# A transformer layer with routed experts: the opening norm stage in a new order, and the first maxima scheduled anew

## The reference, cut to what matters

```python
x = x + _layernorm(attn(_layernorm(x)))          # x is 4 batches x 1024 tokens x 256
x = x + _layernorm(ffn(_layernorm(x)))           # 8 experts, one per token

def attn(x):
    latent = x @ Wc_down                          # 256 -> 128
    q = (latent @ Wq_up).reshape(B, T, 16, 16)    # 16 heads of 16
    k, v = split(latent @ Wkv_up)                 # one key and one value head for all
    att = softmax(causal(q @ k.T / 4))
    return (att @ v) @ Wc_proj

def ffn(x):                                       # logits = x @ centroids.T, argmax picks the expert
    ...
```

## Time and profile before

| | |
|---|---|
| median of 3 runs | 882.81 us (882.48 to 886.35) |
| the profiled execution | 882.63 us, of which 880.9 us span |
| PE busy | 825.6 us (94%) |
| DVE busy | 638.9 us (73%) |
| ACT busy | 550.7 us (63%) |
| POOL busy | 292.9 us (33%) |
| TensorE clock, mean granted | 0.963 of full |
| first maximum on PE | 45.62 us from the span's start |
| first score on PE | 60.60 us |

### The profile page before, as it was taken

One profiled execution on the slowest core, in us unless ns is written; L12 is line 12 of the kernel. 1 busy time (PEld: TensorE's weight loads), 2 busy tenths in 40 slices (PEclk: granted clock), 3 DMA queues, 4 the chain that ended last, 5 costly groups with the idle time before them and its releaser, 6 DMA issues. The chain is left out here.

```text
span 880.9 us, 20297 instructions
## 1 busy us (share of the span) xinstructions
PE 825.6 (94%) x5520; PEld 495.3 (56%) x5521; DVE 638.9 (73%) x2133; ACT 550.7 (63%) x1244; POOL 292.9 (33%) x547
## 2 busy tenths in 40 slices
PE   7999999999999999999999999469999999999993
PEld 3533333333433333433333338369999999999993
DVE  7789889898888898898988607835555555555552
ACT  3624768777766777676776876146666666666661
POOL 4502322443244233432233322042444444444211
PEclk9977999999999999999999999669999999999997
DMA  6111233222311111111143228920000100110000
GB/s 204 42 40 62 80 99 107 76 71 89 106 58 48 40 60 52 55 35 56 56 152 100 71 76 251 334 96 25 30 31 31 35 29 27 36 32 23 21 19 1
DMA packets 55764, 62.92 MB, mean 71 GB/s; under 512 B 13166, under 2 KB 47366, under 8 KB 55568
## 3 DMA queue, kind: packets, MB, share of 16 engines
q1 hardware_dynamic: 51952, 53.71, 18.7%
q0 software_dynamic: 3744, 8.40, 3.1%
HBM read 36.12 MB, written 9.57 MB: 52 GB/s over the span
## 5 line engine op out<-in xcount | busy, mean ns | idle before, releaser
L1066 ACT ACTIVATE W2s<-bank 128x512 f32<-128x512 f32 (+1 forms) x512 | 257.2, 572 | 126.1 <-PE bank L978 123.8
L1116 DVE CUSTOM_DVE_ANT_0 room_kv<-bank,causal 128x384 bf16<-128x384 f32 (+3 forms) x512 | 220.6, 485 | 31.4 <-PE bank L947 29.8
L978 PE MATMUL bank<-W2s,room_kv 99*128 99x512 bf16 (+3 forms) x768 | 225.8, 331 | 5.1 <-ACT W1s L1066 3.3
L947 PE MATMUL bank<-room_kv,W2s 96*128 96x512 bf16 (+3 forms) x768 | 222.8, 336 | 4.3 <-DVE R L1088 3.0
L1119 DVE TENSOR_REDUCE MP<-bank 128x1 f32<-128x512 f32 x256 | 162.9, 680 | 13.6 <-PE bank L947 13.5
L1248 POOL TENSOR_SCALAR_AFFINE_SELECT W2s<-W2s 128x512 f32<-128x512 f32 x96 | 61.2, 637 | 291.4 <-ACT W2s L1066 289.3
L978 PEld LDWEIGHTS bank<-W2s,room_kv 99*128 99x128 bf16 x768 | 68.2, 98 | 146.4 <-ACT W2s L1066 64.6
L1516 PEld LDWEIGHTS hp<-XNT,LT 128*128 128x128 f32 x1248 | 148.0, 195 | 3.7 <-DVE XNT L1593 1.8
L1516 PE MATMUL hp<-XNT,LT 128*128 128x128 f32 x1248 | 148.5, 278 | 1.4 <-DVE XNT L1593 1.4
L1524 PE MATMUL yp<-W2s,LT 128*128 x624 | 141.2, 379 | 0.7 <-DVE z L1605 0.7
L995 PE MATMUL bank<-W2s,room_kv 128*32 128x512 f32 (+2 forms) x1152 | 128.6, 531 | 0.2 <-ACT W1s L1052 0.2
(11 more groups left out here) (185 smaller groups left out, 777.7 us busy)
## 6 DMA issues: line engine op xcount, KB each, us to landing
W2s<-W2s SPq DMA_DIRECT2D x160, 64.0 KB, 2.6
W1s<-in_L_ffn_W_dram SPq DMA_DIRECT2D x8, 1024.0 KB, 5.6
W2s<-in_L_ffn_W_dram SPq DMA_DIRECT2D x8, 1024.0 KB, 7.2
Y<-in_L_attn_x_dram SPq DMA_DIRECT2D x8, 512.0 KB, 6.2
Y<-W1s SPq DMA_DIRECT2D x32, 128.0 KB
W1s<-den_rows SPq DMA_DIRECT2D x16, 256.0 KB
LT<-in_L_attn_x_dram SPq DMA_DIRECT2D x8, 512.0 KB, 6.5
x_rows<-LT SPq DMA_DIRECT2D x8, 512.0 KB, 4.2
```

The costliest lines, as they stand in the source:

```text
L947: last = pe.matmul(bank[:, at:at + w], Q[0:NR, g, i // BW, h, i % BW * P:(i % BW + 1) * P], K[b % 2][0:NR, k * NQ:k * NQ + w], start=True, ...
L978: last = pe.matmul(dst[:, i, :], K[b % 2][0:KR, j * P:(j + 1) * P], Q[0:KR, g, c, h, off:NQ], start=True, stop=True)
L1066: act.activation(PR[t % RB][:, heads[0]:heads[-1] + 1, off:NQ], unit_of(ST[(NU * n + u) % STB], s), ACT.Exp, scale=SCALE).then_inc(exp_don ...
L1116: op = dve.tensor_tensor_reduce(junk[:, done % 2, at:at + w], src, causal[:, NQ - w:NQ], 1.0, LOWEST, ALU.add, ALU.max, dst)
```

## The change

The eight tiles of the norm stage are no longer a loop. Each engine gets a written-out order:

- the norm of tile 1 goes directly behind that of tile 0 and the norm of tile 2 directly behind its statistics; `down` of tiles 0 and 1 follows tile 1's transposes;
- "k" is the first piece and "q00" the second, both after tile 2; "q01" after tile 3, "q10" after tile 4, "q11" after tile 5;
- `XT` has five buffers instead of three;
- `down` of tile 6 goes to before event 4, `x_parts` of batch 2 to before event 7, its `x_fold` to before event 10; `down` of tile 7, `x_parts` and `x_fold` of batch 3 go behind the first scores of round 0 (steps 0, 1 and 2);
- the schedule: 20 maxima before the first score instead of 22, 45 at x = 10 instead of 48, and only at the end of the round the lead of 38; in round 0 an "m" lies 2 maxima behind its chunk's last one instead of 5; the first values lie at 18.2 instead of right behind the first chunk's maxima.

```diff
-FIRST = ("q00", "k", "q01", "q10", "q11")
-FIRST_AT = {2: ("q00",), 3: ("k", "q01"), 4: ("q10", "q11")}
+FIRST = ("k", "q00", "q01", "q10", "q11")
...
-EARLY = 22
+EARLY = 20
+MIDDLE = 45
 MLAT = 5
+FIRST_MLAT = 2
...
     def reached(x):
-        return EARLY + x * (c0 + LEAD - EARLY) / c0 if x < c0 else x + LEAD
+        if x < c0:
+            return EARLY + x * (MIDDLE - EARLY) / c0
+        return MIDDLE + (x - c0) * (c1 + LEAD - MIDDLE) / (c1 - c0) if x < c1 else x + LEAD
...
-            marks.append((NM * r + SET_LAST[c] + MLAT + 0.5, ("m", r, c)))
-    marks.append((SET_LAST[0] + 0.3, ("values", 0, None)))
+            marks.append((NM * r + SET_LAST[c] + (MLAT if r else FIRST_MLAT) + 0.5, ("m", r, c)))
+    marks.append((EARLY - 1.8, ("values", 0, None)))
...
+            statistics(0, 0)
+            statistics(1, 1)
+            inverse(0, 0)
+            norm(0)
+            inverse(1, 1)
+            norm(1)
+            statistics(2, 2)
+            inverse(2, 2)
+            norm(2)
+            statistics(3, 0)
+            centre()
+            remainder("k")
+            remainder("q00")
+            inverse(3, 0)
+            norm(3)
+            remainder("q01")
+            statistics(4, 1)
...
+            turn(0)
+            turn(1)
+            down(pe, 0)
+            down(pe, 1)
+            turn(2)
+            first("k")
+            first("q00")
+            down(pe, 2)
+            turn(3)
+            first("q01")
+            c_turn()
+            down(pe, 3)
+            x_parts(pe, 0)
+            turn(4)
+            first("q10")
+            x_fold(pe, 0)
+            down(pe, 4)
+            turn(5)
+            first("q11")
+            x_parts(pe, 1)
+            down(pe, 5)
+            turn(6)
+            x_fold(pe, 1)
+            turn(7)
...
                 if k == 2:
-                    down(pe, N1 - 1)
-                    x_parts(pe, B - 1)
-                    pe.wait_ge(lx_done, B - 1)
+                    pe.wait_ge(lx_done, B - 2)
                 if k == 3:
-                    pe.wait_ge(lt_copied, N1)
-                if k == FOLD_AT:
-                    x_fold(pe, B - 1)
+                    pe.wait_ge(lt_copied, N1 - 2)
+                if k == LATE_AT:
+                    down(pe, N1 - 2)
+                if k == PARTS_AT:
+                    pe.wait_ge(xt_copied, N1)
+                    x_parts(pe, B - 2)
+                if k == PARTS_AT + 3:
+                    x_fold(pe, B - 2)
                 event(k)
...
+                    if n == 0 and s == 0:
+                        down(pe, N1 - 1)
+                    if n == 0 and s == 1:
+                        pe.wait_ge(lt_copied, N1)
+                        x_parts(pe, B - 1)
+                    if n == 0 and s == 2:
+                        x_fold(pe, B - 1)
```

More of the change, by code:

```diff
@@ L471, in remainder, with norm @@
                 dve.tensor_tensor(rest, bank, parts(name)[0], ALU.subtract).then_inc(first_left, 1)
[L473 to L476, removed]
+            def norm(t):
                 dve.wait_ge(rstd, t + 1)
@@ L480, in norm_vector @@
                     normalise(dve, t, i).then_inc(xn_dve, 1)
[L481 to L491, removed]
+            statistics(0, 0)
[15 more added lines that the diff above has]
+            statistics(4, 1)
+            inverse(4, 1)
+            norm(4)
+            statistics(5, 2)
+            statistics(6, 0)
+            inverse(5, 2)
+            norm(5)
+            remainder("q10")
+            x_logits(dve, 0)
+            statistics(7, 1)
+            inverse(6, 0)
+            norm(6)
+            remainder("q11")
+            inverse(7, 1)
+            norm(7)
+            x_logits(dve, 1)
         def down(pe, t):
@@ L525, in norm_tensor, with turn @@
             pe.wait_ge(w_in, 48)
-            for t in range(N1):
+            def turn(t):
+                past(pe, xt_copied, t - 1)
                 for i in range(QT):
@@ L536, in norm_tensor, with first, c_turn @@
                 last.then_inc(xt_ready, 1)
[L537 to L546, removed]
-                    x_fold(pe, t // 2 - 1)
-                for name in FIRST_AT.get(t, ()):
-                    i, bank, _ = spot(name)
-                    if i == 0:
-                        pe.wait_ge(wq_turned, 1)
-                    pe.wait_ge(lt_copied, QC if name == "k" else int(name[-1]) + 1)
-                    past(pe, first_left, i - 1)
-                    piece(pe, 0, name, bank).then_inc(first_ready, 1)
+            def first(name):
+                i, bank, _ = spot(name)
+                pe.wait_ge(wq_turned, 1)
+                pe.wait_ge(lt_copied, QC)
+                past(pe, first_left, i - 1)
+                piece(pe, 0, name, bank).then_inc(first_ready, 1)
+            def c_turn():
+                pe.wait_ge(c_step, 3)
+                for c in range(DC):
+                    last = pe.transpose(lxp[0][:, c * E:(c + 1) * E], Cn[:, c * P:(c + 1) * P], ident[0:E, 0:E])
+                last.then_inc(c_turned, 1)
+            turn(0)
[22 more added lines that the diff above has]
+            turn(7)
         def norm_scalar(act):
@@ L599, in norm_scalar @@
-            latent(N1 - 1, (N1 - 1) % 2)
-            x_copy(B - 1)
+            turned(0)
+            turned(1)
+            root(2, 2)
+            latent(0, 0)
+            latent(1, 1)
+            turned(2)
+            root(3, 0)
+            first("k")
+            first("q00")
+            second("k")
+            second("q00")
+            latent(2, 0)
+            turned(3)
+            first("q01")
+            root(4, 1)
+            second("q01")
+            c_copy()
+            latent(3, 1)
@@ L602, in attention @@
+            x_copy(0)
+            turned(4)
+            root(5, 2)
+            root(6, 0)
+            first("q10")
+            latent(4, 0)
+            second("q10")
+            turned(5)
+            root(7, 1)
+            first("q11")
+            x_copy(1)
+            second("q11")
+            latent(5, 1)
+            turned(6)
+            turned(7)
+            latent(6, 0)
+            x_copy(2)
+            return latent, x_copy
         PR = [W2s[:, 4 + k, :].rearrange("p (h q) -> p h q", h=GH) for k in range(RB - 1)]
```

100 lines of the change are left out of this document (54 added, 46 removed).

## The result

| | before | changed |
|---|---|---|
| median | 883.43 us (9 runs, 882.48 to 888.41) | 890.00 us (9 runs, 885.15 to 890.13) |
| ratio | | 1.0053, 95% interval 1.0034 to 1.0071 |
| the profiled execution | 882.63 us | 890.07 us (span 888.3) |
| TensorE clock, mean granted | 0.963 | 0.959 |
| first maximum on PE | 45.62 us | 43.00 us |

The change makes the kernel about 0.5% slower; the interval leaves out 1. (The two medians alone are 0.74% apart and the means of the nine runs 0.48%: a median of runs that lie in groups jumps between them.) 882.81 (the median that the forecast was made against) times 1.0053 is 887.5, within the range of 878 to 889; the changed kernel's own median of 890.0 is 1.0 above its end. The forecast of 884.6 had the sign and underestimated the size.

What follows compares the result with a forecast made beforehand. DVE was taken to bound the catching up of the maxima. Start 43.0 + work 50.1 + 0.2 + idle 8.4 put round 0's end at 101.7 against 99.8, 1.9 us later: 884.6 us, range 878.0 to 889.0.

Steps and rivals of the forecast that it cites:

- term 1: End of the norm stage: first maximum on PE at 43.0 us instead of 45.62; bounds 40.3 and 45.6.
- Gap and logit sums (2, 3): DVE's gap at 49.29: 0.4 of 1.80 us stays; batch 2's logit sums behind the maxima: 0.2 more work.
- First "m" (4): Round 0, behind chunk 0's maxima: DVE stops for 0.9 us; bounds 0 and 1.3.
- Values (5): First values, near 56 us: 3.3 us at low clock, DVE idle 1.8 us; bounds 0.1 and 2.0.
- `down` of tile 7 (6): Among round 0's first scores: DVE idle 1.8 us, clock halfway back; bounds 0.1 and 3.3.
- Second "m" (7): Behind chunk 1's maxima: DVE idle 2.1 us in place of 0.26, plus 0.3 for batch 3's logit sums.
- "0.5 stays" (8): Last 8 steps of round 0: three moved maxima fill DVE's idle 1.45 us, of which 0.5 stays.
- Rival 3: Clock stays low through all three float32 pieces among the scores: 889.6 us, chance 0.10.
- Rival 1: Clock stays high through the values and `down`, 0.1 us idle at each: 881.2 us, chance 0.24.
- Rival 2: SP's transfers set the start at 40.3 us and the "m"s cost little: 876.5 us, chance 0.12.
- Rival 4: Start not earlier, at 45.6 us, since DVE's waits for ACT pile up: 887.2 us, chance 0.06.

Runs made afterwards that it cites:

- e9: The changed kernel with round 0's first "m" 5 maxima behind its chunk again, the second still 2: 887.90 us, 1.0029 to the kernel before.
- e5: The changed kernel with round 0's second "m" 5 maxima behind its chunk again, the first still 2: 881.56 us, 0.9967 to the kernel before.
- e1: The changed kernel with both of round 0's "m"s 5 maxima behind their chunks again: 881.38 us, 0.9980 to the kernel before.
- e10: e12 with two extra float32 products on PE ahead of each "m" of round 0: 882.23 us, 0.9977 to the kernel before.
- e12: The changed kernel with both "m"s 5 maxima behind and the values at their old place: 879.52 us, 0.9941 to the kernel before.
- e7: The changed kernel with two extra float32 products on PE ahead of each "m" of round 0: 883.43 us, 1.0004 to the kernel before.
- e4: The kernel before, with its old norm order, given only the new schedule: 888.42 us, 1.0051 to the kernel before.

## Why the prediction was right, and where it was short

**Start (term 1): right, and to the digit by luck.** 43.0 forecast, 43.00 measured, with the keys' first part at 18.05 (18.9 forecast) and SP waiting 3.5 us for "q01" (2 forecast). The forecast lay between 42.3 with the clock high and 43.8 with it low early. The clock did not fall at 13.9, with the new order in no trace; here it fell at 23.7. Where it stayed high in the norm stage, nine traces show 42.05 to 42.30, so the count of the work was good within 0.3 us.

**Gap and logit sums (2, 3): right, if anything too large.** DVE has no wait over 0.3 us between 43.56 and 52.44, for 0.4 forecast.

**First "m" (4): right at its place, short in effect.** Its rows show 0.88 + 0.32 = 1.20 for 0.9; e9 and e5 price it at 1.5 to 2.3 in round 0.

**Values (5): right.** 3.60 us and a wait of 1.90, for 3.3 and 1.8. The clock was low, and that was the step most in doubt. Not foreseen: at the old place they would have covered POOL's chain.

**`down` of tile 7 (6): too large.** 1.8 forecast, 0.76 measured. The clock was back at 64.6, just ahead of it, and the four passes took 1.88.

**Second "m" (7): short.** 1.51 + 1.17 = 2.68 for 2.1 + 0.3. The piece stands behind the "m" and takes 1.46 us, as the clock falls in the middle of it.

**The step that failed** is the one behind term 7: "0.5 stays" (8), with the clock taken as high from the piece on, because before it stayed low only until 75.2 and was 1.00 from 79.65 to 99.80. The second turn left PE idle for 2.17 us up to 74.08, and at 74.90 the clock fell again, for 10.2 us. DVE waited 2.97 there. The forecast had 8.4 us of idle and 50.3 of work; measured were 10.5 and 50.9, so round 0 ended at 104.37 instead of 101.7.

**The second omission** is the last round: "a later stage that changes its length" was named as what would prove the forecast wrong, and one did, by 3.9 us of low clock less about 1.0. Without it, the profiled execution would have been about 886.2 (or 887.2, without what came back too), within the forecast's own range (882 to 887.5). Against the +1.8 of the forecast, round 0 alone shows +4.6: the path was right, its size was not. (882.81 + 1.9 is 884.7, not 884.6; nothing hangs on it.)

**The rivals.** Rival 3 (889.6) comes nearest to the changed kernel's median, but not by its mechanism: it asked for a clock of 0.50 from the values to the piece "q00", and the clock was high for 10.3 us between, for `down` and `x_parts`; only `x_fold` (1.73 us) found it low. Rivals 1, 2 and 4 fell with the clock at 51.0, the start at 43.00 and the two early "m"s.

## What to carry to other kernels

A serial chain through another engine needs as much independent work behind its start as it is long. Moving the turns three maxima earlier, which should bring the scores forward, cost about 2 us at one place and 3 to 4 at the other, and the first score came at 59.34 instead of 57.13 (e1), of which 0.8 is the later start. Filler work ahead of such a chain helps only where the engine would have stood still; elsewhere it makes the hole itself (e10). Where such a hole is on TensorE, price also what its clock does behind it: work that just kept pace at 2.4 GHz is the bound at 1.2. And when a change touches a prologue, add up its effects there first and look for a second place only with the remainder in hand: here it was 400 us later.

## What the hardware showed that was not expected

**Idle is not what the clock needs to fall.** In e12 PE is busy for 8.92 of 9.00 us, and the clock falls at 51.5 all the same; the rows of 42 to 51 and 51 to 65 us:

```profile
42.00:51.00 9.00, 8.92 (x59) 5.26 (x56) 7.54 (x35) 3.50 (x4) 2.21 (x6) 1.00 0.14 48
51.00:65.00 14.00, 11.99 (x36) 4.34 (x36) 12.45 (x29) 3.43 (x7) 0.68 (x2) 0.63 0.01 3
```

The Trainium skill (TensorE: Matmul & The Clock Gate, "Why this matters for your kernels") asks, against such falls in mid-kernel, that PE have no long gaps between bursts. This trace does not agree: PE's rows show no wait from 42.06 on until one of 0.34 at the fall itself. Busy is here what the profile counts as busy: sixteen passes of 16 columns are 1.94 us of it (48.16), and the ends of matmuls are modelled. The changed kernel's own fall at 51.0 does lie in a gap, of 2.44 us, some 1.3 us after it began, so that trace doesn't speak against the rule; it is just not the whole condition.

**More work, less time.** e7's profiled execution has 3.9 us more on TensorE than the change's and ends round 0 5.6 us earlier.

**The same instructions, another clock.** The norm stage is the same code in the changed kernel and eleven of the runs; in these twelve executions the clock fell in it in three, for 3.4 us each, and not in nine; in the kernel before and e4, again with the same norm stage, it was low from 13.9 to 17.3 and from 11.8 to 18.6. The starts move by 0.9 and 1.4 us with it. The last round runs the same list with the same waits of PE ahead in both kernels, at 1.00 in one and 0.50 in the other. What a stretch is granted can't be read from the stretch alone.
